# Fused attention and LoRA-MoE block on one core: a re-ordered head and a re-ordered tail

## The reference, cut to what matters

```python
mod = silu(c) @ wmod                       # c (4,256) -> 6 rows of 256: sa, ca, ga, sb, cb, gb
h = layernorm(x) * (1 + ca) + sa           # x (4, 512, 256)
q, k, v = (h @ (codes * repeat(scales, 32)) + bias)        # 256 -> 16 heads of 128, each
attn = softmax(q k^T / sqrt(128)) v                         # 4 batches, 16 heads, 512x512
x = x + ga * (attn @ wo + bo)              # |ga| at least 0.25
h = layernorm(x) * (1 + cb) + sb
out = h @ W.T + sum over the top 2 of 8 experts of  weight * (h @ A_e.T) @ B_e.T * 16
x = x + gb * out
```

## Time and profile before

| | |
|---|---|
| time, median of 3 runs | 777.44 us (777.26 to 777.73) |
| the profiled execution, its own time | 777.42 us |
| its span, first to last instruction | 775.5 us |
| granted TensorE clock, mean | 0.998 |
| TensorE matmuls busy | 766.5 us, 99% of the span |
| VectorE / ScalarE / GpSimd busy | 647.5 (83%) / 517.6 (67%) / 483.4 us (62%) |
| share of the chain that ended last | TensorE 95%, each other engine and DMA 1% |
| first scores of step 0 start at | 20.43 us |
| end of the last matmul | 772.36 us |

### The profile page before, as it was taken

One profiled execution on the slowest core, in us unless ns is written; L12 is line 12 of the kernel. 1 busy time (PEld: TensorE's weight loads), 2 busy tenths in 40 slices (PEclk: granted clock), 3 DMA queues, 4 the chain that ended last, 5 costly groups with the idle time before them and its releaser, 6 DMA issues.

```text
span 775.5 us, 14722 instructions
## 1 busy us (share of the span) xinstructions
PE 766.5 (99%) x4206; PEld 667.7 (86%) x4206; DVE 647.5 (83%) x1254; ACT 517.6 (67%) x1124; POOL 483.4 (62%) x454
## 2 busy tenths in 40 slices
PE   7999999999999999999999999999999999999998
PEld 6888888888888888888888888888888888888887
DVE  5889888888888888888888888888898888879876
ACT  2788676667666676667666766676667676766841
POOL 4686576548655675556657575655667476789722
PEclk9999999999999999999999999999999999999999
DMA  7554355444454335444445434543355334433202
GB/s 216 162 154 124 95 147 150 139 107 99 118 144 131 95 96 139 129 124 98 110 133 147 98 94 122 146 125 95 96 145 152 95 94 107 112 89 86 56 1 109
DMA packets 71898, 90.67 MB, mean 117 GB/s; under 512 B 19574, under 2 KB 37431, under 8 KB 71867
## 3 DMA queue, kind: packets, MB, share of 16 engines
q1 hardware_dynamic: 53184, 74.00, 37.3%
q10 hardware_dynamic: 18682, 16.30, 7.0%
HBM read 22.06 MB, written 2.11 MB: 31 GB/s over the span
## 4 chain that ended last, share of the span: by engine, by line
PE 95%; POOL 1%; DVE 1%; DMA 1%; ACT 1%; SPq 1%; issue 0%; DVEq 0%
PE score L1102 9%; PE score L1103 9%; PE score L1104 9%; PE qv L1102 8%; PE qv L1103 8%; PE qv L1104 8%; PE o L1102 7%; PE o L1104 7%; PE o L1103 7%; PE ky L1102 4%; PE ky L1103 4%; PE ky L1104 4%; PE y L1102 2%; PE y L1104 2%; PE y L1103 2%; DMA stage<-in_L_attn_wk_scales_dram 1%
## 5 line engine op out<-in xcount | busy, mean ns | idle before, releaser
L404 POOL TENSOR_TENSOR pT_lo<-pT,pT_hi 128x512 fp32r<-128x512 f32 x248 | 314.6, 1305 | 240.7 <-ACT pT_hi L576 240.6
L660 ACT ACTIVATE prob<-score,neg_max 128x512 f32<-128x512 f32 x256 | 172.7, 688 | 79.7 <-DVE neg_max L941 79.5
L941 DVE TENSOR_REDUCE neg_max<-score 128x1 f32<-128x512 f32 x256 | 159.7, 682 | 1.6 <-PE score L1104 1.6
L954 DVE STREAM_TRANSPOSE pB<-prob 128x512 f32<-128x512 f32 x252 | 156.4, 678 | 0.0
L576 ACT ACTIVATE pT_hi<-pT 128x512 fp32r<-128x512 f32 x248 | 135.3, 620 | 0.0
L1102 PE MATMUL score<-k_hi,q_hi 128*128 128x512 f32 x256 | 101.2, 395 | 0.6 <-DVE k_lo L862 0.6
L1103 PE MATMUL score<-k_lo,q_hi 128*128 128x512 f32 x256 | 100.3, 392 | 0.0
L1104 PE MATMUL score<-k_hi,q_lo 128*128 128x512 f32 x256 | 99.7, 389 | 0.0
L1102 PE MATMUL o<-pT_hi,v_hi 128*128 128x512 f32 x248 | 96.6, 389 | 0.0
L1104 PE MATMUL o<-pT_hi,v_lo 128*128 128x512 f32 x248 | 96.5, 389 | 0.0
L1103 PE MATMUL o<-pT_lo,v_hi 128*128 128x512 f32 x248 | 96.5, 389 | 0.0
(11 more groups left out here) (262 smaller groups left out, 1824.7 us busy)
## 6 DMA issues: line engine op xcount, KB each, us to landing
pT<-pB SPq DMA_DIRECT2D x1008, 64.0 KB, 2.0
out_dram<-x_nat SPq DMA_DIRECT2D x8, 256.0 KB, 2.1
stage<-in_L_attn_wv_codes_dram ACTq DMA_DIRECT2D x7, 256.0 KB
stage<-in_L_attn_wv_scales_dram ACTq DMA_DIRECT2D x14, 128.0 KB
stage<-in_L_attn_wq_codes_dram ACTq DMA_DIRECT2D x7, 256.0 KB
stage<-in_L_attn_wq_scales_dram ACTq DMA_DIRECT2D x14, 128.0 KB
stage<-in_L_attn_wk_codes_dram ACTq DMA_DIRECT2D x7, 256.0 KB
stage<-in_L_attn_wk_scales_dram ACTq DMA_DIRECT2D x14, 128.0 KB
```

What stands on the lines that cost most here:

```text
L404: pool.tensor_tensor(split(pT_lo, kt), turned(par, kt), split(pT_hi, kt).bitcast(f32), ALU.subtract).then_inc(p_lo_ok, 1)
L660: act.activation(prob[:, i], score_ps[i][:, :], ACT.Exp, bias=neg_max[:, i:i + 1], accum_out=row_sum[:, s % 2, i:i + 1]).then_inc(exp_ok, 1)
L941: dve.tensor_reduce(neg_max[:, i:i + 1], score_ps[i][:, :], AX.X, ALU.max, negate=True).then_inc(max_ok, 1)
L954: dve.transpose(pB[:, s % 2, :, i].rearrange("p g k q -> p k g q"), prob[:, i].rearrange("p (k g q) -> p k g q", k=QT, g=G)).then_inc(pB_o ...
```

## The change

It touches the head, steps 0 and 1, and the tail. The loop over the middle pairs is as before.

Head: the first scales of q, k and v are no longer loaded repeated. One DMA for each (on ScalarE's queue) brings 4 rows of scales into a zeroed buffer, and TensorE repeats them over 32 partitions each with a matmul (`spread_rows`) against a 0/1 block matrix that VectorE makes; VectorE multiplies codes and scales for q, k and v (`first_product`), where GpSimd did k and v. k comes ahead of q, and both are projected and split in halves of 256 tokens. The modulation columns are made for one half of the features at a time. Runs of identity transposes (`keep_busy`) stand in new places in TensorE's order. The layer norm of batch 1 moves from ScalarE into VectorE's step 0.

```diff
+        def load_rows(queue, m):
+            src = bass.AP(SCALES[m].tensor, 0, [[FEAT, NB], [NB * FEAT, 2], [1, PW]])
+            queue.wait_ge(rows_zero, 1 + "kqv".index(m))
+            queue.dma_start(scale_rows[m][0:NB], src).then_inc(ld_rows[m], 16)
...
@@ block.sync
+            load_first(sp, "k")
             load_first(sp, "q")
-            load_first(sp, "k")
             load_x(1)
...
@@ block.gpsimd
             inverse_std(0)
+            parts("k", 0, 0)
             parts("q", 0, 0)
-            product("k", 0)
-            parts("k", 0, 0)
+            parts("v", 0, 0)
             parts("q", 0, 1)
             inverse_std(1)
-            product("v", 0)
-            parts("v", 0, 0)
             parts("k", 0, 1)
...
@@ block.scalar
+            load_rows(act, "k")
+            load_rows(act, "q")
+            act.wait_ge(c_tr, 1)
+            act.activation(c_exp[:, :], qv_ps[:, 0:B * DC], ACT.Exp, scale=-1.0).then_inc(c_exped, 1)
+            load_rows(act, "v")
...
             for c in range(DC):
+                modulation_out(c)
                 input_high(0, c, score_ps[2 + c])
+            act.wait_ge(h_ev, 2)
+            act.activation(hT_hi[:, 1, tokens(0)], hT32[:, 1], ACT.Copy).then_inc(h0_hi, 1)
...
-            q_high(1, 0)
-            k_high(1, 0)
-            normalise(1, range(QT))
+            for m in "kq":
+                for u in range(2):
+                    half_high(m, u)
...
@@ block.vector
+            for m in "kqv":
+                dve.memset(scale_rows[m], 0.0).then_inc(rows_zero, 1)
...
+            first_product("k")
+            first_product("q")
+            input_hi(0, 0)
+            input_lo(0, 0)
+            dve.wait_ge(ld_x[1], 16)
+            row_statistics(1, 0)
+            row_statistics(1, 1)
+            input_lo(0, 1)
+            first_product("v")
+            row_statistics(1, 2)
+            row_statistics(1, 3)
...
@@ block.tensor
+            def spread_rows(m):
+                pe.wait_ge(block_ok, 1)
+                pe.wait_ge(ld_rows[m], 16)
+                for c in range(2):
+                    ins = pe.matmul(first_scales(m)[:, c], block_rows[:, :, :].rearrange("a b q -> a (b q)"), scale_rows[m][:, c],
+                                    start=True, stop=True)
+                ins.then_inc(rows_mm[m], 1)
+            spread_rows("k")
+            spread_rows("q")
+            keep_busy(4, score_ps[0])
...
+            for u in range(DC):
+                for i, j in enumerate((SA + u, CA + u)):
...
+                ins.then_inc(mod_mm, 1)
+                keep_busy(4, score_ps[0])
+                for t in range(QT):
+                    pe.wait_ge(z_ok, t + 1)
+                    ins = pe.transpose(INPUT_BANKS[0][u][:, t * P:(t + 1) * P], z[:, 0, t, u * P:(u + 1) * P], ident[:, :])
+                ins.then_inc(h_tr, 1)
...
+            keep_busy(4, qv_ps)
+            pe.wait_ge(w_ok["k"], 1)
+            project_halves("k", k_mm)
             pe.wait_ge(w_ok["q"], 1)
+            project_halves("q", q_mm)
```

`dense(1, 0)` went ahead of the transposes of batch 2, and `dense(1, 1)` ahead of `lora_rows(2)`, so that nothing is left between `lora_rows(2)` and the transposes of batch 3. The rest of the tail's diff:

```diff
@@ block.scalar, last step: ahead of v_out
+                    if end:
+                        ffn_input_out(0, 0, o_ps[0])
+                        ffn_input_out(0, 1, ky_ps)
...
@@ block.vector, behind the last step (y_add(n - 2) of the last step is taken out there)
-            for kt in range(QT):
-                end_low(kt)
+            y_add(N - 3, B - 2, 1, False, tiles=range(2))
+            end_low(0)
+            end_low(1)
+            y_add(N - 3, B - 2, 1, False, tiles=range(2, QT))
+            end_low(2)
+            end_low(3)
             o_low(N - 1, ky_ps)
...
@@ block.tensor
             pe.wait_ge(ag_ev, QT * B)
+            dense(3, 1, (2,))
             lora_transpose(0)
-            dense(3, 1)
+            dense(3, 1, (3,))
             lora_transpose(1)
```

More of the change, by code:

```diff
@@ L758, in _ @@
             weighted_lora_out(0)
+            weighted_lora_out(1)
             odds(1)
-            for b in range(1, B):
+            for b in range(2, B):
                 weighted_lora_out(b)
@@ L955, in turn @@
                                       prob[:, i].rearrange("p (k g q) -> p k g q", k=QT, g=G)).then_inc(pB_ok, 1)
-                    if not start:
+                    if not start and not end:
                         v_low(n + 1, batch_of(s) % 2, s % 2)
@@ L963, in pair @@
                     if end:
+                        v_low(n + 1, batch_of(s) % 2, s % 2)
+                        statistics(1)
                         inverse()
-                        statistics(1)
                         o_low(n - 1)
                         prob_low(n - 1, (s - 1) % 2, range(QT))
+                    elif start:
+                        normalise(1, range(2))
+                        v_low(1, 0, 0, ky_ps)
+                        normalise(1, range(2, QT))
+                        q_low(n + 2, head_slice(p, s + 1))
+                        turn(0)
+                        k_low(n + 2, head_slice(p, s + 1))
+                        input_hi(1, 0)
+                        turn(1)
+                        input_hi(1, 1)
+                        turn(2)
+                        turn(3)
+                        inverse()
+                    elif first and s == 1:
+                        dve.wait_ge(ld_x[2], 16)
+                        statistics(2)
+                        turn(0)
+                        turn(1)
+                        q_low(n + 2, head_slice(p, s + 1))
+                        turn(2)
+                        k_low(n + 2, head_slice(p, s + 1))
+                        turn(3)
+                        inverse()
                     else:
@@ L1003, in pair @@
                         statistics(3)
-                    if not early:
+                    if not early and not end:
                         y_add(n - 2, batch_of(s - 2), (s - 2) % 4, first and s % 2 == 0)
@@ L1265, in f_tile, with dense @@
                 return f_banks[2 * b + k // 2][:, (k % 2) * D:(k % 2 + 1) * D]
-            def dense(b, half):
+            def dense(b, half, tiles=None):
                 pe.wait_ge(wg_ok[b], 2)
-                for k in range(2 * half, 2 * half + 2):
+                for k in tiles or range(2 * half, 2 * half + 2):
                     for c in range(DC):
```

214 lines of the change are left out of this document (120 added, 94 removed).

## The result

The changed kernel takes 779.56 us (median of 10 runs, 778.61 to 780.88), the kernel before beside it 777.55 (777.16 to 778.07, 10 runs): ratio 1.0028, 95% interval 1.0020 to 1.0036. It is slower by 2.0 us where 0.1 us less had been forecast, and 779.56 lies above the range, which ended at 779.2. Its ten runs spread over 2.3 us, those of the kernel before over 0.9; in a larger set of 31 runs the kernel before, too, ranges from 776.82 to 779.66.

What follows compares the result with a forecast made beforehand. The prediction took the chain from step 0's last turn through SP's 16 DMAs and `pT_hi` to step 3 as the bound. 777.44 + 0.4 (step 3 later) - 0.5 (tail) = 777.3 us; range 774.4 to 779.2.

Steps and rivals of the forecast that it cites:

- pT chain: Steps 0 to 2: step 0's last turn, SP's 16 DMAs, landing, `pT_hi` and its followers set step 3's start.
- T: End of step 0's last turn on VectorE: forecast 29.2 us, 1.3 later than before.
- TensorE's new waits: Idle of 3.9 us: some 1.6 ahead of v's projection in step 1, 2 to 3 in `weighted(0)` for `pT_lo`.
- S3: Start of step 3's scores: forecast 53.45 us against 53.04 before, +0.4.
- S0: Start of the first scores, after the head: forecast 17.2 us, 3.2 earlier than 20.43.
- T - S0: Step 0, first scores to the last turn's end: 12.0 us forecast, bounds 11.3 to 12.9.
- T to pT_hi, and pT_hi to S3: SP's issues, landing and hold after step 0's last turn, 11.9 us; then `pT_hi` to step 3's start, 12.35 us.
- T decides, not S0: Step 3's start follows step 0's last turn, not the first scores, so the 3.2 us head gain is not passed on.
- The tail: End of kernel: 0.25 of new wait, less idle of 0.59 and a wait of 0.2, gives -0.5 us (-0.8 to -0.2).
- rival C: Head: clock falls to the lower level near 10.8 us, first scores at 19.1, time 779.2 us; chance 0.13.
- Rival B: Steps 0 to 3: chain does not bind or binds late, head's 3.2 us and the tail come through, 773.7 us; chance 0.28.
- Rival D: Tail: idle before batch 2's transposes comes back ahead of `lora_transpose(0)`, no tail gain, 777.8 us; chance 0.11.

Runs made afterwards that it cites:

- second profile of the changed kernel: The changed kernel run once more, nothing altered, against the kernel before: median 779.97 us of 5 runs; the profiled execution took 779.97.
- table of five profiles: Stretches up to step 3 in profiles of the changed kernel (twice), with old tail order, one wait filled, both filled: 778.98, 779.97, 780.21, 783.34, 780.23 us.
- the kernel with both waits filled: Changed kernel plus unused identity transposes in two TensorE waits: 10 ahead of v's projection in step 1, 15 ahead of `weighted(0)` in step 2; 780.04 us.
- the delayed DMAs: Kernel before, with four extra DMAs on SP's queue ahead of step 0's 16 pT DMAs: 779.95 us against 777.69, ratio 1.0024.

## Why the prediction was wrong

The mechanism was right as far as it went: the head's gain doesn't pass the pT chain, T moves back, and TensorE's new waits stand where they were named. One of them was given the wrong releaser (the copy of `o` into `hT`, not `pT_lo`), and a third, 0.6 in step 0, was not listed. What failed are two terms of S3 that were put too small, the tail, and all that was left out of the sum: the second round of SP's queue, and what single executions lose on top. The profiled execution took 778.98, which is still inside the range; the median is outside it by what single executions lose, and for that the sum had no term.

- **The head, S0.** 17.2 forecast, 17.79 measured (17.35 to 20.90 in other profiles of the same head). q's matmuls end at 16.81 for 16.4, and the last high and low parts take 0.98 for 0.6.
- **The step that failed, first: T - S0, mis-sized.** It was put at 12.0 (own bounds 11.3 to 12.9), and measured 12.74. Two z of 0.84 took 2.02, and a cast of 0.42 took 1.12. The rows above show what stood beside them: a GpSimd product of 1.30 from 21.45, and its `hT_lo` of 1.30 from 27.74. With GpSimd at rest the other two z took 0.87 and the other cast 0.43. The Trainium skill ("SBUF — State Buffer", section "SBUF: two separate sides") has VectorE and GpSimd exclude each other there for a whole instruction, for a VectorE operation with two SBUF inputs (against a GpSimd operation that reads SBUF) and for one in a mode that uses two ports. The trace agrees, and I had weighed that rule only for the head's low part, not for the moved layer norm and casts. No run moved the GpSimd work away to test it. The working has a slip as well: the start of `k_lo`, S0 + 8.49, is 8.26 by its own terms (5.9 + 1.67 + 0.69), and the lower bound, 7.8, is 8.1; 8.77 was measured.
- **T to pT_hi, and pT_hi to S3.** 11.9 and 12.35 forecast, 11.55 and 12.28 measured. S3 = 17.79 + 12.74 + 11.55 + 12.28 = 54.36, against 53.45: +1.3 over before instead of +0.4.
- **The step that failed, second: "T decides, not S0", read as ending at S3.** The sum stopped at step 3 and put nothing for the 16 DMAs of step 1, which follow on the same queue with no pause and on which step 4 then stood (`pT_hi` of step 1 waited 1.26 us for them). This added 0.47 in the changed kernel, by one issue of 1.63 us that used up the slack there (0.78 in the kernel before).
- **The tail.** -0.5 forecast, -0.21 measured. The idle of 0.59 went, and 0.27 was the expected new wait (0.25 forecast). The 0.2 in `weighted_end` did not go (`hT_lo`, 0.2 in the list of before and in that of the changed kernel); instead 0.22 ahead of batch 0's `lora_rows` did. "`lora_rows(3)` of 2 x 0.93 and the split `dense(3, 1)` give no wait" was wrong: some 0.3 more went in short pauses around it. The new order alone costs 0.37.
- **The sum of the profiled execution.** 1.83 - 0.21 = 1.62, against a measured 1.56.
- **The clock, rival C, and the last 0.6.** Rival C was given 13 in 100, with its place in the head only, priced through S0. In the second profile of the changed kernel it came as written: 0.50 from 12 to 14 us and S0 19.21, for which C had 19.1. The falls in steps 1 and 2 came behind the very waits that the forecast listed as idle at no further cost. The median lies 0.6 above the profiled execution, which had no fall and no late landing. The table of five profiles shows three things that such an execution can lose, the clock in the head, the clock in steps 1 and 2, and the landing, and each of the other four profiles has at least one of them. How the 0.6 divides among them stays open: the mean clocks of the ten runs don't settle it (the fastest, 778.61, has 0.996, and 779.45 has 1.000), and with the clock up in all six runs the kernel with both waits filled took 780.04. The Trainium skill ("TensorE: Matmul & The Clock Gate", Part 1) says that one and the same kernel has a different number of its first matmuls at the lower clock from run to run. The two profiles of the changed kernel agree (0.50 from 12 to 14 us in one, 1.00 in the other), and show such a difference far behind the start as well: 0.50 between 40 and 43 us in one, 1.00 in the other.
- **Rival B** (the chain doesn't bind) was given 28 in 100 although the rows beside it spoke for the chain; the delayed DMAs exclude it. **Rival D** was the nearer one for the tail, by its size (0 for -0.21) and not by its place: no idle came back ahead of `lora_transpose(0)`.

## What to carry to other kernels

When a stage is started earlier, ask what its slowest consumer is, and follow that chain until it has slack, through every later round of the same queue: here a serial queue of 16 DMAs per step carried a delay of one step into the next. Put the instruction that feeds such a queue first in its engine's order, and the work that has slack behind it: with the turns first in steps 0 and 1, and the layer norm and statistics out of their way, the same head gained 1.9 us; with the turns last it lost 2.0. A wait that you add on TensorE can cost more than its length, since in part of the executions the clock falls behind it; and price an instruction that you move to VectorE by what GpSimd does at the new place.

## What the runs showed of the hardware

- TensorE at 1.2 GHz (granted clock 0.50) for some 4 to 7 us behind waits of 1.2 and 2.9 us in the midst of steady work (from 39 and from 47 us), in some executions and not in others of the same program.
- VectorE's 128x256 normalisation at 0.44 us each with GpSimd at rest, two of them in 2.02 beside a GpSimd product of 1.30; a 128x512 cast at 0.43, and 1.12 beside a GpSimd subtraction.
- `pT` DMAs of 64 KB, issued every 0.65 us, land in 2.0 us; single ones took up to 2.9, 3.2 and 3.5 us in three profiles, and single issues 1.17 to 1.80 us instead of 0.59 in six, each with an instruction transfer of 0.02 MB at that time.
